# Filler matmuls removed from the opening and the two seams of a two-layer cross-attention kernel

## What is computed

```python
# x (8, 56, 256); context (8, 1500, 256); 16 heads of 128
for wq, bq, wk, bk, wv, bv, wo, bo, bias_k, bias_v in two_layers:
    h = layer_norm(x)
    q, k, v = h @ wq + bq, context @ wk + bk, context @ wv + bv
    k, v = append(k, bias_k), append(v, bias_v)          # one extra key and value
    x = x + softmax(q @ k.T / sqrt(128)) @ v @ wo + bo
x = x + gelu(layer_norm(x) @ w_fc1 + b_fc1) @ w_fc2 + b_fc2
```

## Time and profile before

| | |
|---|---|
| median of 3 runs | 1236.87 us (1236.75 to 1239.4) |
| profiled execution, its own time | 1234.94 us |
| its span, first to last instruction | 1233.1 us |
| mean granted clock of PE | 0.999 |
| PE busy | 1210.1 us, 98% |
| DVE, ACT, POOL busy | 833.2, 767.9, 894.0 us |
| filler matmuls (L698) | 108 instructions, three places |

### The profile page before, as it was taken

How to read it: one execution, slowest core, us unless ns; L and a number is a source line. 1 busy time by engine, 2 the same in 40 slices (tenths; PEclk the granted TensorE clock), 3 DMA queues, 4 the chain that set the end, 5 groups by cost and what they waited for, 6 DMA issues and landing times. The chain is left out here.

```text
span 1233.1 us, 26572 instructions
## 1 busy us (share of the span) xinstructions
PE 1210.1 (98%) x7736; PEld 1111.1 (90%) x7736; DVE 833.2 (68%) x1395; ACT 767.9 (62%) x1495; POOL 894.0 (72%) x744
## 2 busy tenths in 40 slices
PE   7999999999999999999999999999999999999998
PEld 6779999999999999998896999999999999999897
DVE  6765767676767676676755666676766666677654
ACT  5746666565666565676484656666666666667655
POOL 5737777777777787679551768686868686867882
PEclk9999999999999999999999999999999999999999
DMA  5401222222222222223320122222222222312231
GB/s 179 126 19 51 56 76 55 74 57 73 61 69 64 67 68 61 59 62 102 103 69 18 38 56 71 61 73 58 74 57 74 58 76 56 79 42 65 73 93 38
DMA packets 147720, 83.60 MB, mean 68 GB/s; under 512 B 121116, under 2 KB 122540, under 8 KB 147672
## 3 DMA queue, kind: packets, MB, share of 16 engines
q1 hardware_dynamic: 147128, 82.27, 25.5%
q10 hardware_dynamic: 544, 0.75, 0.2%
HBM read 68.56 MB, written 0.53 MB: 56 GB/s over the span
## 5 line engine op out<-in xcount | busy, mean ns | idle before, releaser
L607 POOL TENSOR_TENSOR pt<-slots,pt 125x512 fp32r<-125x512 f32 (+3 forms) x384 | 451.0, 1181 | 174.9 <-ACT slots L1069 167.6
L782 PE MATMUL psum<-qs,ctx 128*125 128x384 f32 (+1 forms) x2304 | 537.9, 370 | 3.0 <-ACT slots L1095 2.3
L782 PEld LDWEIGHTS psum<-qs,ctx 128*125 128x125 f32 x2304 | 394.2, 186 | 50.3 <-ACT slots L1095 10.1
L799 PE MATMUL psum<-ctx,pt 125*128 125x258 f32 (+1 forms) x1344 | 382.8, 285 | 1.4 <-ACT on L1076 0.5
L800 PE MATMUL psum<-ctx,pt 125*128 125x256 f32 (+1 forms) x1344 | 379.4, 282 | 0.0
L801 PE MATMUL psum<-ctx,pt 125*128 125x258 f32 (+1 forms) x1344 | 378.9, 282 | 0.0
L1068 ACT ACTIVATE pt<-slots 125x512 fp32r<-125x512 f32 (+3 forms) x384 | 221.3, 576 | 232.9 <-DVE slots L1356 221.9
L1368 DVE TENSOR_TENSOR t_max<-psum,t_max 125x512 f32<-125x512 f32 (+1 forms) x320 | 199.0, 622 | 200.9 <-PE psum L782 200.8
L1095 ACT ACTIVATE slots<-psum 125x512 f32<-125x512 f32 (+1 forms) x384 | 206.5, 538 | 121.7 <-DVE t_max L1368 112.6
L799 PEld LDWEIGHTS psum<-ctx,pt 125*128 125x128 f32 (+1 forms) x1344 | 253.5, 189 | 16.1 <-ACT on L1076 3.5
L800 PEld LDWEIGHTS psum<-ctx,pt 125*128 125x128 f32 (+1 forms) x1344 | 254.2, 189 | 6.7
(11 more groups left out here) (105 smaller groups left out, 972.4 us busy)
## 6 DMA issues: line engine op xcount, KB each, us to landing
nat_stage<-ctx_nat SPq DMA_DIRECT2D x60, 375.0 KB
tr_stage<-ctx_tr SPq DMA_DIRECT2D x60, 375.0 KB, 3.1
w_raw<-weights SPq DMA_DIRECT2D x70, 256.0 KB, 2.7
qt<-turn SPq DMA_DIRECT2D x256, 32.0 KB, 2.0
qt<-turn SPq DMA_DIRECT2D x224, 24.0 KB, 1.9
dk_rest<-dk_rows SPq DMA_DIRECT2D x2, 768.0 KB, 5.7
w_raw<-weights ACTq DMA_DIRECT2D x2, 256.0 KB, 4.6
dk_first<-dk_rows SPq DMA_DIRECT2D x2, 256.0 KB, 4.7
```

The source lines that it names most:

```text
L607: nc.gpsimd.tensor_tensor(split_weights(h, LO, c), logits(h, c), as_f32(split_weights(h, HI, c)), ALU.subtract).then_inc(pt_lo, 1)
L782: last = mm(scores(h, k), ctx_tr_chunk(half, a, c), qs[h][:, m, half, 0:R], start=(half, a, m) == terms[0], stop=(half, a, m) == terms[-1])
L799: mm(out_bank[:, 0:D + 2], hi, ctx_nat_hi(c), start=(c == 0), stop=False, skip_group_check=True)
```

## The change

All 54 filler matmuls go, with the function that issues them, PE's wait for the tile of zeros, and the name of the PSUM bank. The tile shrinks from 128 columns to the one that ACT's first activation reads; everything allocated behind it moves down by 508 bytes in each partition. No other engine's program is touched.

```diff
-        filler = sb("filler", [P, P], F32)
+        filler = sb("filler", [P, 1], F32)
...
-        PICK_BANK, LB_BANK, IDLE_BANK = bank[2], bank[4], bank[1]
+        PICK_BANK, LB_BANK = bank[2], bank[4]
...
-            def keep_busy(n):
-
-                for _ in range(n):
-                    mm(IDLE_BANK[:, 0:P], filler[:], filler[:], start=True, stop=True)
...
             start(pe, "pe")
-            pe.wait_ge(filled, INIT + 1)
-            keep_busy(12)
             pe.wait_ge(tables_in, 16 * N_TABLES)
             norm_transposes(0)
-            keep_busy(4)
             for l in range(LAYERS):
...
                 output_quad(heads + 4 * (QUADS - 1), jobs + 4 * (QUADS - 1), True, False, True)
-                keep_busy(15)
                 norm_transposes(l + 1)
-                keep_busy(4)
```

## The result

The changed kernel has a median of 1240.55 us over 9 runs (1237.82 to 1241.96), the kernel before 1236.87 us over 9 runs (1236.01 to 1240.01). The ratio is 1.0024 with a 95% interval of 1.0014 to 1.0035: slower, by 1.7 to 4.3 us, with 3.0 us in the middle. The two medians are 3.7 us apart, the two means 3.1 (1240.57 and 1237.51). Its profiled execution took 1237.82 us, with a span of 1236.0 us, 2.9 us above the span of before.

What follows compares the result with a forecast made beforehand. PE was taken as the bound, at its high clock of 2.4 GHz. Fillers' own time 0, middle seam 2.0, last seam 1.4 and opening 0.2 sum to 3.6 us: 1236.87 becomes 1240.5 us, range 1237.8 to 1242.9.

Steps and rivals of the forecast that it cites:

- Step 1: Fillers' own time at seams and opening: removing them gains 0, since the norm on DVE and POOL sets the transposes.
- Rival B: Fillers are on the path at the last seam and behind the transposes: 0.45 us gained, 1236.4 us; chance 0.06.
- Step 3: PE's clock falls at each seam left without fillers, with a chance of 0.9 at each.
- Rival A: The clock holds at one seam or both: about 1238.7 us with one falling, 1237.1 with none; chance 0.22.
- C: Low clock outlasts 6.8 us because waits break PE's stretches: 1242.1 to 1243.7 us; chance 0.10.
- Step 4: At the seams, the clock stays low for 4.0 to 6.8 us from the first projection.
- Steps 5 and 6: Low clock's cost at the middle seam, 2.0 us (1.6 to 2.6), and at the last, 1.4 (0.8 to 2.0).
- Step 7: Opening without fillers runs at the low clock but partly covered: 0.2 us late, bounds 0 and 0.5.
- Step 8: The tile of zeros shrunk by 508 bytes costs or gains nothing.
- Step 2: Low clock in dense PE work, read at 1155 us: 1.62 us lost for 3.4 us at the low level.

Runs made afterwards that it cites:

- e5: The kernel before without the 4 fillers behind the transposes of each seam; 1238.46 us, ratio 1.0007.
- e2: The kernel before without the 19 fillers of the middle seam only; 1239.02 us, ratio 1.0013.
- e3: The kernel before without the 19 fillers of the last seam only; 1238.64 us, ratio 1.0010.
- e4: The changed kernel with the tile of zeros kept at 128 columns; 1240.50 us, ratio 1.0022 against the kernel before.
- e11: The kernel before without the 15 fillers ahead of the transposes of each seam; 1238.63 us, ratio 1.0011.
- e7: The kernel before with 7 more fillers at the start of each layer's output stage; 1236.73 us, ratio 0.9992.
- e1: The kernel before without the 16 fillers of the opening, seams keeping theirs; 1238.19 us, ratio 1.0004.
- e13: e12 with no filler in the opening; 1235.94 us, ratio 0.9989 against the kernel before.
- e12: The kernel before with 18 instead of 12 opening fillers, 19 instead of 15 ahead at the middle seam, 7 more per output stage; 1235.95 us.

## Why the prediction was right

The forecast was 1240.5 us and the median 1240.55. The mechanism was right, but the hit to 0.1 us is luck: the steps come to 3.6 us, where the traces show 2.7 at the seams and nothing in the opening.

Step 1, the fillers' own time: right. With nothing ahead of them, the transposes start 0.69 us behind `xn` at both seams (608.58 to 609.27, 1206.07 to 1206.76). The chain's 3.35 us of L698 were cover. Behind the transposes the 0 is right as well: from `xn` to the first projection it is 3.33 and 3.34 us in e5, without the set of four, and 3.33 and 3.34 before. Rival B had no place.

Step 3, the fall: right, and surer than 0.9. Every seam without any filler has a low stretch in its trace, six of six (changed, e2, e3, e4), and so have the two of e11; of the fourteen with the full 15 and 4 or more, one has (e7's middle seam). The runs that left no trace fit: two stretches of 6.83 us take 0.0055 off the mean clock, and each of the nine runs of the changed kernel shows 0.994 or less, as 14 of 94 do before. Rival A is out, and so is C in the form I gave it: each seam had one stretch, and it ended.

Step 4, how long: the mechanism was right, the term too long. I put the rise at 4.0 to 6.8 us behind the first projection. It came 4.3 and 4.1 us behind it in the changed kernel, 4.8 in e2, 5.3 in e3, 3.2 and 3.1 in e4; in the opening it came between 3.1 us (changed, where the terms are 0.37 us apart until 15.7) and 5.9 (e1). What stays the same is the length of the low stretch, 6.82 or 6.83 us at all seams without the 15 fillers; since it begins in the idling or the transposes, up to 3.7 us of it lie ahead of the projection and cost only the 0.2 us of the slower transposes.

Steps 5 and 6: 2.0 and 1.4 us forecast. The middle seam lost 1.81, 1.84 and 1.32 us (changed, e2, e4), the last 0.90, 1.46 and 0.45. The order follows the rise behind the projection: 0.45 us lost at 3.1, 0.90 at 4.1 and 1.46 at 5.3 for the last seam. My lower bounds of 1.6 and 0.8 us were too high, because I had no row for a rise sooner than 4.0. By time alone the seams cost 1.6 and 1.2.

Step 7, the opening: the cover is real. Up to L769 the bare opening loses nothing in four traces of four, so the 0.2 us that I put should have been 0. The mark I had set for it, the first score chunk, was a poor one: that stage scatters by 2.5 us (49.80 to 52.29 us from `xn`).

Step 8: right (e4).

Step 2, the price of the low clock in dense work, was right as a price (1.62 us for 3.41 us at the low level), but not every low stretch pays it. I took the 1.62 us between 1155.24 and 1159.51 as lost. Twelve output matmuls later it had been got back: from the first L843 of that stage to the second it is 1155.24 to 1161.15, 5.91 us, before, and 5.75 us after, at the full clock, since there PE waits for DVE instead. Only 0.16 us stayed lost:

```profile
1157.66 1.67 PE L838 MATMUL psum<-w,cs 128*112 128x256 f32 x12 [0.56 <-DVE cs L1475]
...
1162.69 0.67 PE L743 MATMUL psum<-oth,w 128*128 128x448 f32 x2 [1.12 <-DVE oth L1469]
...
1163.41 1.59 PE L838 MATMUL psum<-w,cs 128*112 128x256 f32 x12
```

In five of the six low stretches at this place DVE's `oth` took about 1.90 us, as here. In the sixth, e2's from 560.71, it took 1.09 us, and there the low clock cost its full price: 5.92 us from L843 to L843, against 4.36 to 4.37 in the traces with a quick `oth` and no low stretch.

```profile
560.59 1.09 DVE L1481 TENSOR_TENSOR oth<-qt,oth 128x896 fp32r<-128x896 f32 x1 [0.15 <-ACT oth L1130]
```

Why the total fits all the same: in the profiled execution the seams cost 0.7 us less than I put and the opening 0.2 less, and the medians, 3.7 us apart, lie further apart than the profiled spans (2.9), the means (3.1) and e4 from its kernel before (3.1). The nine runs of the kernel before happened to have a median of 1236.87 us; its 94 other runs have medians of 1237.45 to 1237.71.

## What to carry to other kernels

A filler that the chain of waits shows on the path may cost nothing: compare the distance from the releaser to the first real instruction where the filler ends early and where it ends late. Before taking fillers out of a gap, find PE's dense work behind the gap; that is where the low clock is paid, 1.55 us for 3.41 us of it where PE set the pace (e2, at 560), and 0.16 where another engine did (before, at 1155). And look at the mean clock over many runs: this kernel with its fillers still had 0.993 to 0.999 in 89 of 94. The two kernels with a few fillers more at the middle seam and in the output stages were 1.5 to 1.8 us faster, by what cause is open, while those in the opening gained nothing.

## What the runs showed of the hardware

The low stretches came in two lengths only, 3.41 to 3.42 and 6.82 to 6.83 us: 25 of them in eleven traces, not counting those that the end of a trace cuts off. The clock fell in gaps too mild to suspect, as at 1155, and behind the opening's fillers: it was at 0.50 from 11.16 in e2 and from 10.53 in e5, where PE had idled for 1.4 and 1.7 us between 24 filler matmuls and the transposes. The record showed 1.00 ahead of its first change, though, with matmuls of the low level's length; the mean clock of 1.000 in e13 hides a slow opening for this reason.

The scatter of the time has a second source that is not the low stretches: the eleven runs of e13, all with a mean clock of 1.000, lie between 1234.22 and 1237.32 us. The traces show one candidate. At the start of each output stage the distance from the first L843 to the second is 4.36 or 4.37 us in 8 of 26 cases, 5.75 to 5.77 in 12, and 5.90 to 5.92 in the 6 with a low stretch. DVE's `oth` and POOL's `pm` start there within 0.03 us of each other. Either DVE's first takes 1.09 us and POOL's 1.86 (9 cases, e2's low one among them), or DVE's takes about 1.90 and POOL's about 0.93 (17 cases). In e7 DVE is quick and POOL's two take 3.60 us; in e12 POOL's take 2.67 and DVE's 1.90 and 2.48, and PE waits 1.15 us for it.

```profile
1159.06 1.09 DVE L1481 TENSOR_TENSOR oth<-qt,oth 128x896 fp32r<-128x896 f32 x1 [0.15 <-ACT oth L1130]
1159.08 3.60 POOL L666 TENSOR_TENSOR pm<-p,mask 80x448 fp32r<-80x448 f32 x2
...
1160.66 1.23 DVE L1481 TENSOR_TENSOR oth<-qt,oth 128x896 fp32r<-128x896 f32 x1
```

```profile
1155.37 1.90 DVE L1481 TENSOR_TENSOR oth<-qt,oth 128x896 fp32r<-128x896 f32 x1 [0.15 <-ACT oth L1130]
1155.39 2.67 POOL L666 TENSOR_TENSOR pm<-p,mask 80x448 fp32r<-80x448 f32 x2
...
1157.79 2.48 DVE L1481 TENSOR_TENSOR oth<-qt,oth 128x896 fp32r<-128x896 f32 x1
...
1160.32 0.67 PE L748 MATMUL psum<-oth,w 128*128 128x448 f32 x2 [1.15 <-DVE oth L1481]
```

The Trainium skill ("GPSIMD Engine Reference", 8, "Key points") says that GpSimd shares its SBUF interfaces with VectorE, and that VectorE instructions with two SBUF inputs contend with it; these durations agree, as one engine's gain is the other's loss. Which of them wins goes with the kernel: with the 7 fillers in the output stage (e7, e12, e13) DVE is quick in 5 of 6 cases, without them in 4 of 20. How PE's fillers would bring that about is not shown. A quick DVE is worth 1.4 us in each of two stages (5.76 against 4.36); with 5 of 6 instead of 4 of 20 that is an estimated 1.8 us, as much as e12 and e13 gained; that makes it a rival of the clock there, and no run tests it. That it is part of the run-to-run scatter is argued from the traces as well.
